# Up products of two shared chunks moved from the shared stage into the router stage of a fused attention and mixture-of-experts kernel

## The reference

```
n = layernorm(x)
aff = sigmoid(n @ wa)                                  # [tokens, 16]
top 2 of 16 experts per token, their shares divided by their sum
expert(n) = (gelu(n @ g + gb) * (n @ w1 + b1)) @ w2 + b2      # 512 -> 256 -> 512, gelu exact
out = x + n + sum over 2 shared experts of expert(n) + sum over the token's 2 routed experts of share * expert(n)
```

## Time and profile before

| what | us |
|---|---|
| median of 3 runs (1127.23 to 1128.54) | 1128.45 |
| the profiled execution, its own time | 1127.35 |
| its span, first to last instruction | 1125.6 |
| router stage, about | 719.0 to 756.4 |
| shared stage, about | 756.4 to 865.7 |
| expert stage, about | 865.7 to the end |
| PE busy, share of the span | 1012.7, 90% |
| DVE busy, share of the span | 840.9, 75% |
| POOL busy, share of the span | 598.7, 53% |

### The profile page before, as it was taken

How to read it: one execution, slowest core, us unless ns; L and a number is a source line. 1 busy time by engine, 2 the same in 40 slices (tenths; PEclk the granted TensorE clock), 3 DMA queues, 4 the chain that set the end, 5 groups by cost and what they waited for, 6 DMA issues and landing times. The chain is left out here.

```text
span 1125.6 us, 24931 instructions
## 1 busy us (share of the span) xinstructions
PE 1012.7 (90%) x9303; PEld 751.4 (67%) x9303; DVE 840.9 (75%) x1469; ACT 670.1 (60%) x1166; POOL 598.7 (53%) x645
## 2 busy tenths in 40 slices
PE   5999998679997999968999989659997999999996
PEld 4777776634443667647788867457674888888883
DVE  5589999869998787767778777798747555555547
ACT  4575773679887555658788866354543444554531
POOL 5444445424445345448888787553883455555520
PEclk8999999889999999969999999759998999999998
DMA  8574431859887222342233332364996567668878
GB/s 323 175 261 125 158 124 38 157 159 235 232 220 191 95 67 100 88 130 49 70 81 79 80 85 105 142 236 173 206 282 236 169 230 240 245 234 291 310 273 335
DMA packets 133514, 197.77 MB, mean 176 GB/s; under 512 B 67798, under 2 KB 67964, under 8 KB 132600
## 3 DMA queue, kind: packets, MB, share of 16 engines
q1 hardware_dynamic: 117064, 152.60, 44.3%
q0 software_dynamic: 8544, 24.68, 6.9%
q10 hardware_dynamic: 7792, 18.96, 5.2%
HBM read 129.05 MB, written 46.05 MB: 156 GB/s over the span
## 5 line engine op out<-in xcount | busy, mean ns | idle before, releaser
L470 PE MATMUL ps_y<-kv,toep 128*128 128x288 f32 x640 | 156.8, 407 | 3.2 <-PEq L173 1.9
L470 PEld LDWEIGHTS ps_y<-kv,toep 128*128 128x128 f32 x640 | 121.1, 190 | 38.3 <-DMA toep<-taps_padded 3.2
L164 POOL TENSOR_TENSOR kv<-kx 128x1024 f32<-128x1024 f32 x32 | 60.6, 1894 | 84.1 <-DVE outT L524 37.6
L1847 DVE TENSOR_REDUCE at_negmax<-ps_s 128x4 f32<-128x1024 f32 x64 | 78.1, 1220 | 34.4 <-PE ps_s L1898 33.8
L2759 POOL DMA_INDIRECT expert_results<-e_yo,target x47 | 70.1, 1491 | 55.6 <-ACT e_yo L2810 55.6
L1141 PEld LDWEIGHTS ps_eg<-e_xT,e_w 128*128 128x128 bf16 x1128 | 69.0, 100 | 15.1 <-issue 2.6
L1141 PE MATMUL ps_eg<-e_xT,e_w 128*128 128x128 bf16 x1128 | 73.1, 223 | 4.1 <-DVE e_xT L2871 4.1
L1141 PE MATMUL ps_eu<-e_xT,e_w 128*128 128x128 bf16 x1128 | 72.0, 221 | 0.0
L2864 DVE COPY e_w<-expert_weights 128x4096 bf16 x47 | 57.7, 1227 | 18.3 <-issue 18.3
L2754 POOL DMA_INDIRECT e_rows<-token_rows,token x45 | 43.6, 970 | 50.9 <-PE ps_ex L2970 45.0
L2877 DVE SCALAR_TENSOR_TENSOR e_y<-ps_eu,e_bias,e_y 128x128 f32<-128x128 f32 x94 | 28.6, 346 | 55.1 <-PE ps_eu L1141 54.3
(11 more groups left out here) (457 smaller groups left out, 3025.0 us busy)
## 6 DMA issues: line engine op xcount, KB each, us to landing
e_parts<-down_parts SPq DMA_DIRECT2D x47, 512.0 KB
w_raw<-in_L_ffn_w ACTq DMA_DIRECT2D x32, 512.0 KB, 4.4
toep<-taps_padded SPq DMA_DIRECT2D x32, 256.0 KB, 3.7
f_draw<-in_L_ffn_rw SPq DMA_DIRECT2D x16, 512.0 KB, 4.4
down_parts<-f_dparts SPq DMA_DIRECT2D x16, 512.0 KB, 2.9
expert_weights<-expert_results SPq DMA_DIRECT2D x16, 512.0 KB, 11.1
qs<-r_raw SPq DMA_DIRECT2D x72, 64.0 KB, 2.0
x_res<-in_x SPq DMA_DIRECT2D x4, 1024.0 KB
```

The costliest lines, as they stand in the source:

```text
L164: pool.tensor_tensor(pairs[:, :, :, 0:HD0], x[:, :, 0:HD0].unsqueeze(2).broadcast_to([P, ROWS_N, WIDE, HD0]), sliding_rows(x, 0, 1, WIDE), ...
L470: last = pe.matmul(y[:, l * B:(l + 1) * B, :, WIDE - 1:], toep[h % 2][:, (DC - 1 - l + m) * P:(DC - l + m) * P], kv[h % 2][:, m * B:(m + 1 ...
L1847: dve.tensor_reduce(negmax[u % 2][:, :].rearrange("p (j q) -> p j q", j=2), psS[:, :, :, :], AX.X, ALU.max, negate=True).then_inc(max_read, 1)
```

## The change

Two of the six chunks of the shared stage, 0 and 1, are treated in another way. Their tiles 0 to 3 are turned first in the router as before, but stay in SBUF (`made_xT`) and aren't stored. The router makes their up products, gelu, gate and halves in four units (chunk 0 or 1, shared expert 0 or 1), each of two groups of 24 products, placed between the tiles: up(n, 0) after score(3 + 3n), up(n, 1) after score(4 + 3n). The result stays in SBUF (`y_made`). For this the split of the shared weights is spread anew: ACT makes the first two highs, POOL the other four, DVE all six lows. `TURNS` goes from 3 to 2, since the products need PSUM.

In the shared stage the order of the chunks is 6, 0, 7, 1, 2, 3. Up products are made for 6, 7, 2 and 3 (`UPS`), and for 0 and 1 (`MADE`) only the down products, behind up(i, 1). The places of x are four, only the first chunk's x is loaded by the router, and the others by SP in the shared stage. The experts are spread over four rounds in place of six (`FIRST_E`), and SP's list is written out anew. The diff, cut:

```diff
-X_PLACE = (0, 1, 2, 2, 0, 1)
+X_PLACE = (0, 1, 0, 1, 2, 3)
-EARLY = [CH - 2, CH - 1] + list(range(CH - 4))
+EARLY = [CH - 2, 0, CH - 1] + list(range(1, CH - 4))
+UPS = (0, 2, 4, 5)
+UP_N = len(UPS)
+MADE = (1, 3)
-FIRST_E = [0, 3, 5, 8, 11, 13, 16]
+FIRST_E = [0, 3, 7, 12, 16]
-TURNS = 3
-VECTOR_TILES = (4, 7, 10, 13)
-VECTOR_LOWS = {9: 0, 12: 1}
+TURNS = 2
+UNITS_MADE = len(MADE) * SH_N
+VECTOR_TILES = (4, 8, 12)
+VECTOR_LOWS = {0: 0, 1: 1, 3: 2, 4: 3, 10: 4, 13: 5}
...
         @block.gpsimd
-            for n in range(6):
+            for n in range(2, 6):
                 pool.tensor_copy(place(n, 0), raw[n][:, :]).then_inc(w_high, 1)
...
-            for n in range(len(VECTOR_LOWS), 6):
-                pool.wait_ge(w_high, n + 1)
-                pool.tensor_tensor(place(n, 1), raw[n][:, :], place(n, 0), ALU.subtract)
...
         @block.vector
+            def gate(n):
+                e = n % SH_N
+                dve.wait_ge(gelu_done, n + 1)
+                dve.wait_ge(u_psum, n + 1)
+                for f in range(F2):
+                    at = ROWS["sb1"] + 2 * e + f
+                    last = dve.scalar_tensor_tensor(gf[e][:, f, :], psU[:, f, :], k.vectors[:, at:at + 1], gf[e][:, f, :], ALU.add, ALU.mult)
+                last.then_inc(y_full, 1)
+            def hidden_lows(n):
+                hi, lo = (a[:, n % SH_N, :, :] for a in y_made[n // SH_N])
+                dve.wait_ge(y_high, n + 1)
+                dve.tensor_tensor(lo, gf[n % SH_N][:, :, :], hi, ALU.subtract).then_inc(y_low, 1)
...
                 if t in VECTOR_LOWS:
                     weight_lows(VECTOR_LOWS[t])
+                for n in range(UNITS_MADE):
+                    if t == 6 + 3 * n:
+                        gate(n)
+                    if t == 7 + 3 * n:
+                        hidden_lows(n)
+            hidden_lows(UNITS_MADE - 1)
             dve.wait_ge(exped, 1)
...
         @block.tensor
+            def up(n, m):
+                made, e = n // SH_N, n % SH_N
+                pe.wait_ge(w_low, 2 * e + m + 1)
+                pe.wait_ge(x_high, (made + 1) * ST)
+                pe.wait_ge(x_low, (made + 1) * ST)
+                if n:
+                    pe.wait_ge((gelu_done, y_full)[m], n)
+                for f in range(F2):
+                    for c in range(DC):
+                        col = c * FE + f * P
+                        last = three_products(pe, (psG, psU)[m][:, f, :], [sgu[:, s, e, m, col:col + P] for s in range(2)],
+                                              [made_xT[made][:, :, h, c * P:(c + 1) * P] for h in range(2)], c == 0, c == DC - 1)
+                last.then_inc((g_psum, u_psum)[m], 1)
...
                 score(t)
+                for n in range(UNITS_MADE):
+                    if t in (3 + 3 * n, 4 + 3 * n):
+                        up(n, t - 3 - 3 * n)
...
         @block.scalar
+            act.wait_ge(front.wa_loaded, 16)
+            act.activation(wa_parts[:, 0, :, :], wa[:, :, :], ACT.Copy).then_inc(wa_high, 1)
             act.wait_ge(xn_ready, 2)
             normalise(2)
-            normalise(3)
...
+            for n in range(2):
+                act.activation(place(n, 0), raw[n][:, :], ACT.Copy).then_inc(act_w_high, 1)
+                if n == 0:
+                    normalise(3)
...
+                for n in range(UNITS_MADE):
+                    if t == 5 + 3 * n:
+                        gelu(n)
+                    if t == 6 + 3 * n:
+                        hidden_highs(n)
             act.wait_ge(logits, NT)
             act.activation(ex[:, :, :].rearrange("p t e -> p (t e)"), psL[:, :], ACT.Exp, scale=-1.0).then_inc(exped, 1)
...
 stage_route_and_shared, SP's list:
+            load_raws(0, RAW_N)
+            load_x(1)
...
+            load_raws(7, 14)
+            store_tiles(0)
+            load_raws(14, 16)
+            load_x(2)
+            load_raws(16, 18)
+            store_tiles(1)
+            load_x(4)
+            load_raws(18, 20)
+            load_x(3)
+            load_raws(20, 22)
+            store_tiles(2)
+            load_raws(22, 27)
+            store_tiles(3)
+            load_x(5)
+            load_raws(27, 30)
+            sp.wait_ge(scattered, 16 * 2 * NT)
+            sp.dma_start(table[:, :, :], table_dram.rearrange("(j p) w -> j p w", p=BLK)).then_inc(table_loaded, 16)
+            load_raws(30, 32)
+            store_tiles(CN - 2)
...
 stage_route_and_shared, DVE:
+            for i in range(1, UP_N):
+                left_over = list(experts_of(i - 1))[2:] if i > 1 else []
                 gate(i, 0)
...
                 gate(i, 1)
                 up_lows(FIRST_E[i])
                 low_part(i, 1)
+                up_lows(FIRST_E[i] + 1)
+                if UPS[i - 1] + 1 in MADE:
+                    add_sums(UPS[i - 1] + 1)
...
 stage_route_and_shared, PE:
-            for i in range(1, CN):
+            for i in range(1, UP_N):
...
                 up(i, i % 2, 0)
-                down(i - 1)
+                down(UPS[i - 1])
                 pe.wait_ge(y_full, i * SH_N)
                 up(i, i % 2, 1)
+                if UPS[i - 1] + 1 in MADE:
+                    down(UPS[i - 1] + 1)
             down(CN - 1)
```

More of the change, by code:

```diff
@@ L2093, in stage_router @@
         wa_parts = sb("r_wap", [P, 2, DC, E_N], BF16)
-        turned = [kept[q // ST][:, q % ST, :, :].rearrange("p s (c t) -> p s c t", c=DC) for q in range(SETS)]
+        tile_of = lambda places, q: places[q // ST][:, q % ST, :, :].rearrange("p s (c t) -> p s c t", c=DC)
+        turned = lambda t: tile_of(made_xT, t) if t < MADE_TILES else tile_of(kept, t % SETS)
         ex = sb("r_exp", [P, NT, E_N], F32)
@@ L2116, in _ @@
             sp.wait_ge(front.mid_stored, 16 * NT)
-            for i, chunk in enumerate(KEPT_CHUNKS):
-                for s in range(ST):
-                    sp.dma_start(x_places[i](s), mid_dram[chunk * ST + s, :, :]).then_inc(x_back, 16)
+            for s in range(ST):
+                sp.dma_start(x_place(s), mid_dram[EARLY[0] * ST + s, :, :]).then_inc(x_back, 16)
             sp.wait_ge(bias_set, 1)
@@ L2269, in _, with stage_route_and_shared @@
             act.activation(down_bias[:, :], bias_raw[:, :], ACT.Copy).then_inc(bias_high, 1)
-def stage_route_and_shared(k, xaff, sgu, sd, down_bias, xT, W, bias_rows, expert, token, target, weight, e_rows, e_yo, fetched, late_shares, x_places, gain, shift_parts):
+def stage_route_and_shared(k, xaff, sgu, sd, down_bias, xT, W, bias_rows, expert, token, target, weight, e_rows, e_yo, fetched, late_shares, x_places, gain, shift_parts, y_made):
     nc = k.nc
@@ L2365, in stage_route_and_shared @@
         x_tile = lambda i, s: x_places[X_PLACE[i]](s)
-        x_uses = lambda i: [n for n in range(i + 1) if X_PLACE[n] == X_PLACE[i]]
+        loads_of = lambda i: sum(1 for n in range(1, i + 1) if X_PLACE[n] == X_PLACE[i])
         experts_of = lambda i: range(FIRST_E[i], FIRST_E[i + 1])
@@ L2391, in store_x, with load_raws, store_tiles @@
                 sp.dma_start(mid_dram[EARLY[i] * ST + s, :, :], x_tile(i, s)).then_inc(x_stored[s], 16)
-            for n in range(RAW_N):
-                load_raw(n)
+            def load_raws(first, last):
+                for n in range(first, last):
+                    load_raw(n)
+            def store_tiles(i):
+                for s in range(ST):
+                    store_x(i, s)
+            load_raws(0, RAW_N)
+            load_x(1)
             sp.wait_ge(table_set, 2)
@@ L2612, in raw_highs @@
                 act.activation(W_half(n, 0), raw_at(n), ACT.Copy).then_inc(raw_high, 1)
-            for i in range(CN):
+            for i in range(UP_N):
                 halves = range(2 * FIRST_E[i], 2 * FIRST_E[i + 1])
```

135 lines of the change are left out of this document (76 added, 59 removed).

## The result

The kernel after takes 1153.31 us (median of 4 runs, 1149.66 to 1154.21), the kernel before 1127.84 us in the same measurement (4 runs, 1126.98 to 1128.54). The ratio is 1.0218, with a 95% interval of 1.0199 to 1.0237. The forecast was 1144.0 with a range of 1133 to 1153: slower, as foretold, and 9.3 us more than the likeliest case. That is the very end of the range: 1153.31 is 0.3 us past it, and the ratio on the prediction's own 1128.45 us would give 1153.05.

The account below looks back on a forecast made before the run. It took PE to bound the shared stage and DVE the router. Router +14.7 and shared stage +1.1 made 15.8 on the profiled 1127.35, 1143.2; the runs' median is 1.1 higher: 1144 us, range 1133 to 1153.

Parts of the forecast that it names:

- The router: Router stage: PE's added up groups and a table load before the exponential lengthen it by 14.7 us, bounds +11 to +17.
- rival (b): Router: PE's clock stays at half, so turns and groups take 18.3 us more, 1162 in all; chance 0.07.
- the term +1.1: Shared stage: gives back nothing of PE's 21.0 us and ends 1.1 us later, bounds -4 to +6.
- piece 29 still stands before the table: it is issued at 842.5: SP's queue, shared stage: the table's load goes out behind raw piece 29, at 842.5 on the old scale as before.
- make SP wait for the landing of a store: SP's queue, shared stage: x loads 2 and 3 wait for stores; without PE's pause as cover, 3 to 10 us each.
- The landing: Shared stage: the table lands 4.0 us after its load's issue, bounds 2.9 and 8.2, so at 846.5.
- The chain behind the turn: End of the shared stage: from the table's landing through raw piece 31 to the last add_sums and store, 20.3 us.
- So PE bounds the shared stage: Shared stage before the change: PE, busy 50.9 of 54 us at full clock, sets the pace.
- the table can't be there: Shared stage: PE could reach the table at 831.7 or some 3 us later, but must idle some 12 us for it.
- rival (c): Shared stage bound by PE alone: gives back all 21.0 us against the router's 14.7, so -6.3, 1122; chance 0.07.
- (a): End of the shared stage: chain behind the table stays 13.0 us, stage gives back 6.2, whole +8.5, 1137; chance 0.15.
- (d): Both stages: router grows by 11 and the shared stage gives back about as much, no change; chance 0.03.

Follow-up runs that it names:

- e8: e6 with even rounds, the up rounds beginning at experts 0, 4, 8, 12, 16 in place of 0, 3, 7, 12, 16; 1137.31 us, ratio 1.0051 to the kernel before.
- e7: e6 with the gate low halves that POOL made between its scatters moved to DVE; 1144.40 us, ratio 1.0120 to the kernel before.
- e12: The kernel after with half the rows of 21 raw pieces not loaded, all waits kept; 1151.08 us, ratio 1.0159 to the kernel before.
- e1: The kernel after with the table's load ahead of raw piece 27 in SP's queue; 1143.77 us, ratio 1.0097 to the kernel before.
- e6: e1 with the last round reordered on ACT and DVE so that piece 31's place frees earlier; 1143.15 us, ratio 1.0120 to the kernel before.
- e4: The kernel after with 6 products in place of 24 in each of the router's up groups; 1145.38 us, one run.
- e9: The kernel before with 6 of 24 products in the up groups of two shared-stage chunks, nothing added to the router; 1132.08 us, ratio 1.0040.
- e2: The kernel before with the table's load moved ahead of raw piece 27; 1130.07 us, ratio 0.9994.
- e5: The kernel before with no shared weight split on POOL: ACT makes all six highs, DVE all six lows; 1122.54 us, ratio 0.9923.
- e3: The kernel after with identity in place of gelu in the router's units, so no function table switch there; 1153.04 us, ratio 1.0196 to before.

## Why the prediction was right, and where it was off

**The router.** Right within 2.7 us. up(0, 0) began 14.0 us into the stage (14.5 by the working, from 719.0 to 733.5), the later groups took 2.6 each to the next start, and the exponential ran right behind a table load of 1.28. The clock was 0.98, so rival (b) is out. The largest part of the gap is the first group: 3.0 us to the next start in place of 4.7, because the clock rose inside it. In e8 it took 3.09 and the router 49.4, in e7 3.73 and 50.0, in e12, e1 and e6 4.62 to 4.69 and 50.9 to 51.0. The start of that group gives another 0.5 us, and the last 0.5 I can't assign to one term. e4 confirms that PE sets this length.

**The shared stage.** Right in sign and in its first reason, that PE's 21 us don't come back; the term +1.1 was mis-sized and measured +12.5, twice its upper bound of +6. Three steps failed:

- "piece 29 still stands before the table: it is issued at 842.5". I took over the time of the earlier trace rows, and asked only who releases piece 29. Even in the kernel before it was not gate_lows(11) that released it: SP had stood for 11.3 us for a store's landing, until 840.24, and then issued an x load and pieces 27 and 28 one behind the other, until 842.01; gate_lows(11), which piece 29 needs, had ended at 841.87. Ahead of it in SP's queue piece 27 now waits for a store's landing, since the third x place lies in its room, and piece 28 for up_lows(10). The table went out 6.9 us later. The prediction did say that x loads 2 and 3 "make SP wait for the landing of a store" and that without PE's pause as cover each such wait is worth 3 to 10 us on the table, and then costed them at nothing; piece 27's own wait for a store it did not name. e1 takes the table past them and gives back 8.2 us.
- The landing, 4.0 from bounds of 2.9 and 8.2: 6.6 in after, 4.3 to 7.7 in e1, e6, e7, e8 and e12. With the step before, the turn was at 99.7 and not 90.0.
- The chain behind the turn: 22.1, not 20.3. Its form was right, piece 31 goes out 12.0 us behind the turn as foretold; the group at half clock took 5.3 and not 4.7, and from the end of the last add_sums (889.89) to the expert stage (891.80) it is 1.9 and not 0.84.

The turn was 9.7 us and the chain 1.8 us above the working, together 11.5; the term was short by 11.4.

**How much was luck.** The direction was earned: both halves of the argument, a router that grows by PE's groups and a shared stage that gives nothing back, are what the runs show. The size was not. The time lies outside the forecast's own range of 1138 to 1150, and it stands at the end of the wide one only because that was drawn wide and the router came out 2.7 us cheaper than its term.

**"So PE bounds the shared stage"** was wrong as it stood. e9 takes 16 us of PE's work out and the stage is 2.6 longer. PE was busy for 50.9 of 54 us, but DVE's slots and SP's queue with its landings ran beside it and were as long: PE comes behind them at nearly the same time in e9 as in the kernel before, 31.1 and 31.2 us after the stage's start, then 88.2 and 87.8. "the table can't be there" was the right doubt about the wrong wait: in e9 the x loads' chain took the gain before the table could. This also speaks against rival (c), more strongly than the earlier trace rows did.

**The rivals.** (a), a chain of 13 us behind the turn, did not happen: even e8 has 17.4. (d) asked for a shared stage that gives back the router's growth; the most that any version of the change gave back is 2.5 us.

**Open.** How much of e12's lower ratio is the chip, why e4's shared stage grew by 2.9 us, why a scatter lands after 4.3 us in one run and 8.2 in another, and what paces the transfers while the scatters are under way. A kernel with the change in which SP waits for no store's landing was not tried, nor scatters made earlier without more work on DVE.

## What to carry to other kernels

Before costing a step at "issued when it was before", walk its queue upwards and ask of every entry what it waits for now; an in-order queue passes on the latest wait of all entries. An engine at 94% busy is not a lone bound until work has been taken from it: cutting products in place (e9) costs one line and would have priced the whole benefit of this change at nothing. A place in a queue that costs nothing in one kernel (e2) can cost 8 us in the next (e1), when the entries ahead of it wait for something new.

## What the runs showed of the hardware that was not expected

- With POOL's casts and subtractions taken away DVE finished more instructions in less busy time, 29.6 us for 58 against 35.1 for 53 (e5).
- With half-size pieces the DMA engines' share was 0.97 at 175 GB/s, against 1.03 at 273 (e12 and after), and from the issue of a chunk's store (two of 256 KB) to the end of the wait for it still 10.9 us, against 11.7.
- A scatter whose issue ended at 848.7 counted as landed at 855.87, 7 us later (e1); in e6 it was 8.2 us and in e8 4.3.
- The first group behind a low-clock stretch of the router took 3.13 us in after, 3.09 in e8, 3.73 in e7, and 4.62 to 4.69 in e1, e3, e6 and e12, with the same instructions, by when the clock rose.
